# Unread matrix products at both ends of a fused recurrent-attention and expert kernel, with W2, slot marks, gathers and first loads moved

## What is computed

```python
mix = x + xx * time_maa_x                      # xx: previous token minus this one
lo = tanh(mix @ maa_w1); xm = x + xx * (lo @ maa_w2 + time_maa)   # four mixtures
r, k, v = xm[0] @ Wr.T, xm[2] @ Wk.T, xm[3] @ Wv.T
...                                            # decay w, kk, a, gates g from low-rank products
s = s * w + (s @ a) * b + v * k                # per token, per head
y = s @ q
out = ((norm(y) + rk * v) * g) @ Wo.T          # then added to x and layer-normed: x1
e = argmax(x1 @ centroids.T)                   # one expert per token
z = x1 + relu(norm(x1) @ W1[e] + b1[e]) @ W2[e] + b2[e]   # then doubled residual and normed
```

## Time and profile before

| | us |
|---|---|
| median of 3 runs | 1126.1 (1120.03 to 1128.91) |
| the profiled execution, its own time | 1132.21 |
| its span, first to last instruction | 1130.2 |
| PE busy | 1002.5 (89%) |
| DVE busy | 789.9 (70%) |
| POOL busy | 680.8 (60%) |
| ACT busy | 547.7 (48%) |

### The profile page before, as it was taken

The page is one execution under the profiler, slowest core; times in us unless marked ns, Lnnn a source line. Parts: engine busy times, 40 slices in busy tenths (PEclk is TensorE's granted clock), DMA queues, the critical chain, the costliest instruction groups (busy, mean ns, idle before and its releaser), DMA issues.

```text
span 1130.2 us, 42039 instructions
## 1 busy us (share of the span) xinstructions
PE 1002.5 (89%) x16550; PEld 817.9 (72%) x16551; DVE 789.9 (70%) x1777; ACT 547.7 (48%) x1120; POOL 680.8 (60%) x1138
## 2 busy tenths in 40 slices
PE   4777999999999999999999998766299999999995
PEld 2546777777777777767867777653289898898894
DVE  3576797877879888768978887161566666666663
ACT  4464685665757766656856866221022222222221
POOL 1077988986888888878879889830123233233321
PEclk9678899988989999989999999585599999999998
DMA  4014033242242242241341341328744454554430
GB/s 100 12 37 82 16 87 87 32 95 52 57 105 56 53 105 54 55 105 30 79 97 30 87 96 24 84 58 277 289 152 166 173 181 150 174 178 146 172 126 4
DMA packets 208622, 111.99 MB, mean 99 GB/s; under 512 B 172364, under 2 KB 191952, under 8 KB 208080
## 3 DMA queue, kind: packets, MB, share of 16 engines
q1 hardware_dynamic: 204720, 101.31, 33.3%
q0 software_dynamic: 3744, 8.40, 2.2%
HBM read 85.42 MB, written 26.08 MB: 99 GB/s over the span
## 4 chain that ended last, share of the span: by engine, by line
PE 76%; DMA 7%; DVE 7%; issue 5%; ACT 2%; SPq 2%; POOL 0%; DVEq 0%; ACTq 0%; POOLq 0%
PE bank L551 20%; PE bank L866 12%; PE bank L879 8%; PE bank L633 6%; PE bank L686 6%; PE bank L641 5%; PE ry L879 4%; PE bank L596 4%; PE ry L714 2%; PE ry L663 2%; DMA scr_n<-arena 2%; PE bank L703 2%; DMA arena<-scr_n 2%; DVE arena L1378 1%; PE bank L584 1%
## 5 line engine op out<-in xcount | busy, mean ns | idle before, releaser
L1787 POOL TENSOR_TENSOR arena<-arena 128x30 f32<-128x30 f32 (+14 forms) x480 | 293.7, 612 | 36.4
L551 PE MATMUL bank<-arena 128*128 128x256 f32 (+2 forms) x992 | 294.2, 438 | 23.5 <-DVE arena L1262 10.1
L1790 POOL TENSOR_TENSOR arena<-arena 128x30 f32<-128x30 f32 (+14 forms) x480 | 285.8, 595 | 37.6
L551 PEld LDWEIGHTS bank<-arena 128*128 128x128 f32 x992 | 188.5, 214 | 79.9 <-issue 37.6
L866 PEld LDWEIGHTS bank<-arena 128*128 128x128 f32 x1248 | 147.5, 194 | 4.5 <-DVE arena L1686 2.6
L866 PE MATMUL bank<-arena 128*128 128x128 f32 x1248 | 148.1, 278 | 2.0 <-DVE arena L1686 2.0
L1378 DVE TENSOR_TENSOR arena<-bank,arena 128x512 f32<-128x512 f32 x128 | 79.4, 682 | 40.9 <-PE bank L633 40.6
L1192 ACT ACTIVATE arena<-arena 128x1 f32<-128x1 f32 x39 | 11.5, 295 | 177.6 <-DVE arena L1650 177.6
L879 PE MATMUL bank<-arena 128*128 x416 | 96.4, 385 | 0.1
L1818 POOL COPY arena<-arena 128x1 int32 (+1 forms) x39 | 7.1, 181 | 146.2 <-DVE arena L1714 146.2
L641 PE MATMUL bank<-arena 128*128 128x128 f32 x576 | 89.7, 296 | 5.3 <-DVE arena L1439 3.3
(11 more groups left out here) (167 smaller groups left out, 1672.2 us busy)
## 6 DMA issues: line engine op xcount, KB each, us to landing
arena<-in_W SPq DMA_DIRECT2D x47, 1024.0 KB, 5.0
scr_n<-arena SPq DMA_DIRECT2D x64, 128.0 KB, 2.8
arena<-scr_n SPq DMA_DIRECT2D x16, 512.0 KB, 4.6
scr_u<-arena SPq DMA_DIRECT2D x16, 512.0 KB, 2.9
arena<-scr_u SPq DMA_DIRECT2D x64, 128.0 KB, 2.9
arena<-in_xTp SPq DMA_DIRECT2D x32, 132.0 KB, 4.0
arena<-in_x SPq DMA_DIRECT2D x64, 64.0 KB, 2.1
scr_x<-arena SPq DMA_DIRECT2D x64, 64.0 KB, 2.9
```

Source lines behind the costliest of these rows:

```text
L551: mm = pe.matmul(ring.tile(m, name)[0:rows, to], lhsT, rhs, start=(i == 0), stop=(i == len(terms) - 1))
L1787: inv_ok.inc(f"m{s}", TT(t, U[:, 0:s, s:s + 1].broadcast_to(shape), U[:, s:s + 1, s + 1:TB].broadcast_to(shape), ALU.mult))
L1790: inv_ok.inc(f"a{s}", TT(U[:, 0:s, s + 1:TB], U[:, 0:s, s + 1:TB], t, ALU.add))
```

## The change

Products that nobody reads are put at 26 places of PE's order: `warm_up` multiplies a zeroed tensor, `keep_busy` multiplies the identity by a loaded weight, 256 columns each, into a bank that nobody reads then (`ry_bank[0]` in bodies -2 to 0, `idle_ps` from body 16 on). Their counts are 12 in body -2, 23 in body -1, 23 in body 0, 12 in body 16, 11 in body 17, 2 in body 18 and 42 around the routing table. Bodies 1 to 15 get none. Besides:

- `par`, `maa1T`, `maa2` are issued by ACT (`first_in`), and the first operations wait for those and x alone; `masks`, `mats` stay on SP. The two scaled matrices are made later in DVE's body -2. ACT loads one table at once and none in body -2.
- All seven groups of slots, and the ranks before them, move on DVE to the end of body 16, behind both copies of the solved x.
- SP loads the last tokens before it writes the last inverse, and issues W2 right behind the last inverse's transfers, ahead of the last two x1 stores.
- The first three gathers take their indices from the table itself, without a copy on POOL.
- DVE's first `relu` stands behind `keep_xnT(1)`.

```diff
@@ SP
-            early = [(par, d["par"]), (w_maa1, ...), (w_maa2, d["maa2"]),
-                     (masks, d["masks"]), (mats, ...)]
+            early = [(masks, d["masks"]), (mats, ...)]
...
+                if n == last + 1:
+                    load_tokens(last)
                 if has(n - 1):
                     inverse_to_heads(n - 1)
+                if n == last + 1:
+                    load_experts()
...
-                if n - 1 == last:
-                    load_tokens(last)
-                    load_experts()
@@ PE
+            def warm_up(count):
+                for _ in range(count):
+                    pe.matmul(ry_bank[0][:, 0:2 * P], Ux_flat[:, 0:P], Ux_flat[:, 0:2 * P], start=True, stop=True)
+            def keep_busy(count, out):
+                for _ in range(count):
+                    pe.matmul(out[:, 0:2 * P], ident, w_sq[:, 3, 0, :], start=True, stop=True)
...
                 if n == last + 1:
                     rank_known()
+                if n == last + 1:
+                    ring.wait_empty(pe, last, "x1")
+                    keep_busy(4, idle_ps)
                 if has(n - 1):
                     solve(n - 1, 1)
...
-            pe.wait_ge(early_in, 80)
-            pe.wait_ge(const_ok, 10)
+            pe.wait_ge(clear_ok, 1)
+            warm_up(4)
+            pe.wait_ge(first_in, 48)
+            pe.wait_ge(const_ok, 8)
...
             route_pe.inc("rank", ...)
+            keep_busy(14, idle_ps)
...
+                if n == NTILE // 2:
+                    keep_busy(3, idle_ps)
...
             route_pe.inc("table", mm)
+            keep_busy(25, idle_ps)
@@ ACT
+            for dst, src in ((par, d["par"]), (w_maa1, ...), (w_maa2, d["maa2"])):
+                act.dma_start(dst, src).then_inc(first_in, 16)
+            nc.scalar.preload_act_table_set("sigmoid_and_others")
@@ DVE
-                if n == last + 1:
-                    place_known()
-                    mark_slots(0, 3)
                 if has(n - 1):
                     keep_x_odd(n - 1, 1)
-                if n == last + 1:
-                    mark_slots(3, 6)
...
                 if n == last + 1:
-                    mark_slots(6, 7)
+                    place_known()
+                    mark_slots(0, KNOWN // GROUP)
...
-                    relu(0, 0)
                 keep_xnT(j)
+            relu(0, 0)
@@ POOL
+                if isinstance(j, int) and j < DEPTH:
+                    index = table[:, j:j + 1]
```

More of the change, by code:

```diff
@@ L782, in body @@
                     norms(n + 1)
+                if -1 <= n <= 0:
+                    keep_busy(1, ry_bank[0])
+                if has(n + 1):
                     square(n + 1, "r", 0, 0)
@@ L792, in body @@
                     turn_values(n, 0)
+                if n == 0:
+                    keep_busy(3, ry_bank[0])
+                if has(n):
                     turn_values(n, 1)
@@ L801, in body @@
                     read_out(n - 1, 1)
+                if n == last + 1:
+                    keep_busy(2, idle_ps)
                 if has(n + 1):
@@ L1112, in body @@
                     keep_x1T(n - 3)
-                if n < last:
+                if -2 < n < last:
                     sigmoid_tables()
@@ L1807, in gather @@
             def gather(j, s):
-                if not (isinstance(j, int) and j < DEPTH):
+                if isinstance(j, int) and j < DEPTH:
+                    index = table[:, j:j + 1]
+                else:
                     prep.wait(w, j - DEPTH, "zb")
-                idx_ok.inc("gather", nc.gpsimd.tensor_copy(gidx[:, s:s + 1], table[:, bass.ds(j, 1)]))
-                idx_ok.wait(w, j, "gather")
+                    index = gidx[:, s:s + 1]
+                    idx_ok.inc("gather", nc.gpsimd.tensor_copy(index, table[:, bass.ds(j, 1)]))
+                    idx_ok.wait(w, j - DEPTH, "gather")
                 nc.gpsimd.indirect_dma_start(out=xg[:, s], out_offset=None, in_=x_rows,
-                                             in_offset=bass.IndirectOffsetOnAxis(ap=gidx[:, s:s + 1], axis=0),
+                                             in_offset=bass.IndirectOffsetOnAxis(ap=index, axis=0),
                                              bounds_check=NTOK - 1, oob_is_err=False).then_inc(gathered[s], 16)
```

74 lines of the change are left out of this document (63 added, 11 removed).

## The result

Over 22 runs each the changed kernel takes 1116.2 us at the median (1105.7 to 1122.9), the kernel before 1124.2 (1111.8 to 1139.4). The ratio is 0.9936, with a 95% interval of 0.9912 to 0.9960: about 7 to 8 us faster, where the sum said 21. The median lies inside the range of 1096 to 1120, but 11 us above the 1105.

The account below looks back on a forecast made before the run. PE's work was taken to bound the middle, and a PE, ACT, DVE chain at low clock the ends. Start 12 + end 9 = 21 us off the profiled 1132.2, or 1126.1 - 21 = 1105 at the median; range 1096 to 1120.

Parts of the forecast that it names:

- The marks named for it: Signs of being right: block 0's scores near 36.3 us, inverses near 52.5 and 94, clock 1, faster `read_out`, norm products, `first_layer`.
- marks of "wrong": Signs against: unread products of 0.9 us, PE waiting for body 1's inverse, issue waits over 3 us beside W2, longer middle.
- The start: Up to block 1's scores: earlier first product and higher PE clock save 13.6 us, taken as 12, bounds 5 and 14.
- The third rival: Unread products don't lift the clock and run at 1.2 GHz, 0.945 us each; 1174 us, chance 0.06.
- The middle: Blocks between the ends: PE bounds it and keeps the lead; change costed at nothing, 4 us allowed to both sides.
- The end: From block 15's solve on: 3.0 + 6.7 - 3 + 0.3 + 2 = 9.0 us less, bounds 0 and 13.
- The clock's terms: At the end: full PE clock takes 6.7 us off 767.9 to 791 us, and 2 off the first `first_layer`.
- W2: Issued early, worth nothing as a transfer; delays PE's instruction fetches at `read_out`, 0 to 7.6 us, taken as 3 lost.
- The step of 3.0 for the slots: Slot marks gone ahead of DVE's copy after block 15's `solve`: `read_out` starts at 759.4, not 762.41, 3.0 us less.
- W2 collides: Clock holds, but instruction waits under full DMA cost 7.6 us, not 3, and cool PE; 1112 us, chance 0.10.
- The clock is only half held: High clock in only half of the stretches, clock terms halve; 11 us gained in all, 1115 us, chance 0.17.
- The rule on hidden fetches: Instruction fetches hide behind execution, W2 meets nothing, the 2.53 us wait goes; 1099.5 us, chance 0.10 with a luckier middle.

Follow-up runs that it names:

- e17: e16 without the unread products of the end (bodies 16 to 18 and around the table); 1119.2 us, ratio to before 0.9932.
- e1: The changed kernel again, unaltered; 1120.5 us, ratio to before 0.9924.
- e2: Only the start of the change, with its unread products, and the end of the kernel before; 1117.5 us, ratio to before 0.9930.
- e9: The kernel before on the first 128 of 512 tokens of each sequence (4 blocks); 417.2 us.
- e14: e2 on 320 tokens of each sequence (10 blocks); 777.2 us, where the kernel before takes 793.3.
- e7: The kernel before again, unchanged; 1126.6 us, ratio to before 0.9978.
- e18: e16 again, unaltered; 1109.0 us, ratio to before 0.9827.
- e15: The changed kernel with the load of the last tokens behind the last inverse's transfers, ahead of W2; 1118.1 us, ratio to before 0.9911.
- e5: The changed kernel without any unread product, all moves kept; 1129.4 us, ratio to before 1.0010.
- e3: The changed kernel with W2 and the last tokens' load at their old place, after body 16; 1115.1 us, ratio to before 0.9870.
- e8: e3 with the three row loads (ln_g, ln_b, b2) issued ahead of W2; 1114.7 us, ratio to before 0.9838.
- e16: e8 with W2 in halves, the second behind the last x1 store and the first three W1; 1112.1 us, ratio to before 0.9875.
- e4: The changed kernel without the start's unread products (bodies -2 to 0); 1119.0 us, ratio to before 0.9887.
- e12: The changed kernel on 320 tokens of each sequence (10 blocks); 783.4 us, where the kernel before takes 793.3.
- e10: The changed kernel on 128 tokens of each sequence (4 blocks); 410.2 us, where e9 takes 417.2.

## Why the prediction was right and wrong

**The direction and the mechanism of the clock were right; the end's queue and waits were not.** The marks named for it came: 36.23, inverses at 52.06 and 92.49 (52.5 and 94 written), clock 1.00 in the start, `read_out` 0.87 behind `solve`, the variance product near 1.1, `first_layer` 3.84 with PE busy up to `turn_x`. The centre product, for which 1.1 was written too, took 1.92. And two marks of "wrong" came as well: a wait on issue of over 3 us beside W2 (4.94), and in the trace of after PE waits 2.77 us for the inverse in body 1, where the trace of before shows 0.92 for ACT. (e17 shows the second too, with 2.50; e1 and e2 do not.)

**The start: 12 us, by the runs 8 to 12.** Traces show more, about 14 at the second and third inverse; the three lengths give 9.6, 16.1 and 11.6 by medians, the last 7.9 by its ratio. The third rival, unread products at 1.2 GHz and 1174 us, is out: only the first eight records were cold.

**The middle: 0, with 4 to both sides.** "The lead is kept through the middle, as PE bounds it" leaves POOL out. The nine traces with the lead show 3.4 us more between third and sixteenth inverse and 3.5 more of waiting for inverses. Both are inside the bound given, and the first inside the scatter. That the lead would shrink block by block, which I took up after the result, was not borne out (e9 to e14).

**The end: a gain of 9 us; by the runs of 16 blocks about nothing, by the traces a gain of 3.** This is the step that failed. The means of before and e7, and of after and e1, put each term to its place:

| stretch | forecast | measured |
|---|---|---|
| last inverse to the end of `read_out` | 0 (slots -3.0, W2 +3) | +4.9 (56.9 to 61.8) |
| to the routing | -6.7 | -5.2 (24.1 to 18.9) |
| to the first gather | -0.3 | -0.7 |
| to the end | -2 | -1.8 |
| sum | -9.0 | -2.8 |

The clock's terms came out nearly whole: 7.7 of 9.0 in these traces, and 10 us when e17 and e18 change the unread products alone. What is missing lies ahead of `read_out`'s end. The same traces split that first row:

| part of the first row | forecast | measured |
|---|---|---|
| `solve` starts later | +1.5 | +2.7 (42.9 to 45.5) |
| its products take longer | 0 | +2.5 (4.1 to 6.6) |
| waits on issue in `solve` and `read_out` | +3 | +3.9 (2.8 to 6.6) |
| wait for DVE's copy | -4.5 | -4.1 (5.0 to 0.9) |
| sum | 0 | +4.9 |

The largest miss is the clock in `solve`. I put the four unread products ahead of it against a wait of 0.43 us and took its products at full speed, with no term for what a longer wait would do. The wait behind them was 2.54 and 2.64, and the first 100 products took 5.54 and 4.22 (e1, granted clock 0.69) where 98 had taken 3.07:

```profile
742.97 4.22 PE L692 MATMUL bank<-arena 64*64 64x32 f32 x100 [2.64 <-DMA arena<-scr_u]
```

Second, the load of the last tokens, which the diff moves ahead of the last inverse, has no term in my sum at all, although I had it in the order that I printed: the inverse's way out starts 1.4 us behind POOL's end in after and 3.4 in e1, and e15, with the load moved, starts `solve` 2.2 earlier and has its first 100 products in 3.10 us. That the late inverse is the whole cause of the cold `solve` is not shown: e2, e5 and e17 wait 2.2 to 2.8 us for an inverse that leaves at POOL's end. Third, *W2* was sized by halving my own bounds, "so I stay in the lower half: 3 us lost", and cost about 4, so this term is off by 1. The step of 3.0 for the slots was 4.5 of wait less 1.5 of unread products; the wait gave 4.1 of it.

**The rivals.** *W2 collides*, 1112, came nearest in mechanism. It priced what is added to the waits at 7.6; 3.9 was added (to 6.2 and 7.0 in all). It had PE cooled by them, so that centre and variance run cold: centre did (1.92 in after, 1.45 in e1), variance did not, and the larger loss of the clock was in `solve`. That W2's early place does it is shown by kernels that differ in SP's order alone: after, e1 and e15 wait 6.2 to 7.0 in all, e3, e8, e16 and e18 between nothing and 2.9. As a transfer I had called W2 "worth nothing" to those behind it. In the change itself that holds; in e3 it is the rows, and W1 behind them, that stand behind it, in e8 the last store, for some 5 and 6 us. *The clock is only half held*, 1115, fits the number best and the chip least. *The rule on hidden fetches*: the 4.94 us, with one packet of the instruction queue in them, are against it. By the Trainium skill, "Runtime: NRT & Kernel Launch", section "Instruction fetch mechanics", the next 16 KiB come mostly behind execution. In these strings of small products that holds in some traces (no wait in e3 and e18) and not in others (2.20 to 2.65 us in before, e7, e8 and e16, 4.94 in after and e1).

**What stays open.** At 16 blocks the start is worth 8 and the changed end about nothing on top, which makes the 7 to 8 of the runs. But in the traces of 16 blocks the sum is larger (14 at the third inverse, 3 back in the middle, 3 at the end: 14), and the runs' 8 does not reach it. e2 shows this most: lead and tail of its trace would make 20 us and more, its runs make 8. The scatter of the middle, 555 to 575 us between third and sixteenth inverse from execution to execution, is as large as what is looked for, and no kernel here settles it. How much of e2's short tail (410.6) is the place of the fetch boundary, and how much the order of W1 and the first gather, was not tried apart either; nor was the changed kernel with that boundary moved and nothing else, which would say whether the changed end can gain its 9 us as it seems to in e4.

## What to carry to other kernels

Unread products in an engine's waits can be priced as the product of a stretch's busy time and its missing clock. At the end that came out (10 to 14 measured for 8.7, uncertain by 7). At the start the runs price products and moves only together (8 to 12 for 12); what the products alone give there is too little for the runs to tell. A big transfer moved within one queue has three prices that have to be looked up one by one: what it meets while it flies (here PE's instructions), what is moved ahead along with it (here a token load, ahead of the last inverse), and who stands behind it wherever it is put; cut in halves, with the small urgent transfers between, it showed none of the three in e16 and e18. And where single executions of one kernel differ by 10 us, two profiled ones must not be subtracted: measure stretches from a common event, such as the last inverse, and ask for them in a second trace.

## What the hardware showed that I had not expected

- The wait for instructions in `read_out` comes in several sizes. With W2 at its old place it is 2.53 and 2.25 us in before and e7, 2.20 in e8, 2.65 in e16, and not there in e3 and e18, though e18 is e16's kernel. With W2 early it is 4.94 in after, e1, e12 and e15 and 4.98 in e10, but 0.67 in e4 and 2.27 in e5, where the DMA is as full (348 GB/s in the wait):

```profile
758.96 1.50 PE L720 MATMUL ry<-arena 128*32 128x32 f32 x94 [0.88 <-DVE arena L1472]
762.74 0.69 PE L720 MATMUL ry<-arena 128*32 128x32 f32 x34 [2.27 <-issue]
```

So a full DMA is not enough for the long wait, and one trace is not enough to say that a kernel has the short one.
- Dense work ahead of a wait does not always carry the high clock over it. `solve` stands behind four unread products in all of these: its first 100 products took 5.54 us after 2.54 of waiting (after) and 4.22 after 2.64 (e1), but 3.1 after 1.04 (e8), 1.03 (e15) and 0.15 (e16). The line is not sharp: all 128 took 5.16 us after 0.99 (e4) and 5.68 after 1.16 (e18), where before needs 4.1.
- The changed kernel's mean granted clock over its runs is 0.956, before's 0.919, and within either kernel a higher clock goes with a shorter run (correlation of clock and span -0.80 over 22 runs, -0.75 over 23). The clock of a whole run is thus no measure of a change: it rose by 0.037 and the time fell by 0.7%. Most likely that is because unread products fill waits with records at speed that nobody needed.
